# L0's attention as one pipeline over all 64 heads, with double buffers and normalizations on ScalarE

## The reference, cut to what matters

```python
a  = tanh(einsum('ble,hde->blhd', emb, Wa_w) + Wa_b)
bg = einsum('ble,hde->blhd', emb, Wb_w) + Wb_b
# for each head and feature, over the tokens of a sequence:
h  = a[t] * h + bg[t]                     # hs, starts at 0 for each sequence
Dx  = emb @ D_w.T + D_b
out = (einsum('blhd,hkd->blhk', hs, C_w) + C_b) * Dx
out = layernorm(out) * hn_g + hn_b        # per head and token
sum_heads = (Dx + einsum('h,blhd->bld', head_w, out)) / nH
z = sum_heads @ Wout_w.T + Wout_b
u = z + layernorm(z) * norm_g + norm_b
h_out = u + gelu(u @ ffn1_w.T + ffn1_b) @ ffn2_w.T + ffn2_b
y = h_out @ proj_w.T + proj_b             # added to x
```

## Time and profile before

| | us |
|---|---|
| median of three runs | 1402.25 |
| lowest and highest | 1392.26, 1405.36 |
| the profiled execution | 1405.92 |
| its span, first to last instruction | 1404.2 |
| PE, DVE, ACT, POOL busy in the span | 1120.8, 932.8, 672.8, 614.1 |
| mean granted TensorE clock | 0.875 |

### The profile page before, as it was taken

How to read it: one execution, slowest core, us unless ns; L and a number is a source line. 1 busy time by engine, 2 the same in 40 slices (tenths; PEclk the granted TensorE clock), 3 DMA queues, 4 the chain that set the end, 5 groups by cost and what they waited for, 6 DMA issues and landing times. The chain is left out here.

```text
span 1404.2 us, 17282 instructions
## 1 busy us (share of the span) xinstructions
PE 1120.8 (80%) x4972; PEld 814.7 (58%) x4972; DVE 932.8 (66%) x2659; ACT 672.8 (48%) x1242; POOL 614.1 (44%) x695
## 2 busy tenths in 40 slices
PE   5767999966787888798776756899992777999997
PEld 4645878854555565565553545788881444555553
DVE  6647887756787777777754634877773368676662
ACT  3324767743344445345342212677770434455532
POOL 5763000016866776674551754100006466664340
PEclk8659999997999999999996667999996589899997
DMA  7537467731000000000000110577751000000000
GB/s 241 189 113 278 143 209 246 245 100 27 12 12 10 12 11 12 10 12 1 1 1 1 38 38 32 178 226 247 239 196 54 23 18 16 23 23 12 8 8 23
DMA packets 48959, 115.43 MB, mean 82 GB/s; under 512 B 8160, under 2 KB 14304, under 8 KB 48864
## 3 DMA queue, kind: packets, MB, share of 16 engines
q1 hardware_dynamic: 40672, 97.53, 21.3%
q0 software_dynamic: 8192, 16.79, 4.0%
HBM read 79.16 MB, written 35.13 MB: 81 GB/s over the span
## 5 line engine op out<-in xcount | busy, mean ns | idle before, releaser
L642 DVE TENSOR_TENSOR hid_lo<-hid,hid_hi 128x512 fp32r<-128x512 f32 x248 | 170.4, 689 | 102.5 <-ACT hid L442 91.4
L491 POOL DMA_INDIRECT xs<-spare_all,slots x128 | 131.5, 1027 | 72.9 <-issue 36.5
L521 POOL DMA_INDIRECT got<-ys,y_slots x64 | 74.8, 1169 | 199.8 <-DMA ys<-spare_all 183.2
L1068 DVE TENSOR_TENSOR_SCAN spare_all<-spare_all,carry 128x512 f32<-128x512 f32 x64 | 90.9, 1420 | 71.3 <-ACT spare_all L972 67.0
L982 ACT ACTIVATE gate_b<-bank,head_rstd 128x128 f32<-128x128 f32 x256 | 72.9, 369 | 126.4 <-POOL head_rstd L1022 124.5
L442 ACT ACTIVATE hid<-bank,b_up_of 128x512 f32<-128x512 f32 x184 | 125.5, 682 | 6.0
L219 PEld LDWEIGHTS bank<-ident,spare_all 128*128 128x128 f32 x568 | 78.2, 157 | 82.8 <-issue 74.5
L219 PE MATMUL bank<-ident,spare_all 128*128 128x128 f32 x568 | 96.3, 302 | 33.2 <-DVE spare_all L551 13.7
L441 ACT ACTIVATE hid_hi<-bank,b_up_of 128x512 fp32r<-128x512 f32 x138 | 95.1, 689 | 44.8 <-PE bank L364 34.6
L908 PE MATMUL bank<-spare_all,cw_sb 128*128 128x512 f32 x128 | 71.6, 642 | 33.4 <-DVE spare_all L1075 33.4
L1029 POOL TENSOR_TENSOR t_sb<-t_sb,gate_b 128x512 f32<-128x512 f32 x64 | 87.8, 1373 | 0.6
(11 more groups left out here) (267 smaller groups left out, 3020.3 us busy)
## 6 DMA issues: line engine op xcount, KB each, us to landing
wr<-wq SPq DMA_DIRECT2D x92, 512.0 KB, 4.4
spare_all<-xs SPq DMA_DIRECT2D x46, 256.0 KB, 4.6
ys<-spare_all SPq DMA_DIRECT2D x46, 256.0 KB, 4.9
wq<-wr SPq DMA_DIRECT2D x16, 512.0 KB
got<-in_w_mlp SPq DMA_DIRECT2D x9, 512.0 KB
xs<-X SPq DMA_DIRECT2D x16, 256.0 KB
xs<-spare_all,slots POOLq DMA_INDIRECT x128
out_x<-X SPq DMA_DIRECT2D x8, 256.0 KB, 2.3
```

Of the source, the lines that this page charges most:

```text
L491: g.indirect_dma_start(out=xs, out_offset=bass.IndirectOffsetOnAxis(ap=slots[:, k, n:n + 1], axis=0), in_=xn_all[:, n], in_offset=None).th ...
L521: nc.gpsimd.indirect_dma_start(out=rows_of(i, ring)[:, k, b], out_offset=None, in_=ys, in_offset=bass.IndirectOffsetOnAxis(ap=y_slots[:, k ...
L642: v.tensor_tensor(hid_lo[:, q], hid[:, n % HC], hid_hi[:, q].bitcast(F32), ALU.subtract).then_inc(s["lo_done"], 1)
L1068: v.tensor_tensor_scan(hs[:, n % 2], a_sb[:, n % 2], b_sb[:, n % 2], carry[:, n:n + 1], ALU.mult, ALU.add).then_inc(s["hs_ready"], 1)
```

## The change

`turn_of` with its eleven slots is gone. One loop over `MIX_SLOTS` = 64 + 13 slots runs on each engine, and head q = 8 i + h is projected in slot q whatever its tile. Each slot holds the work of heads n, n-1, n-2 and n-3. The work of a tile hangs on `phase` = n % 8, for the tile itself, the one before it, and the one two before (f2, h, y and X of tile i-2 now stand in phases 0 to 4 of tile i).

- Two buffers for `x_hi`/`x_lo` (the halves of `xh` and `xl`), `dx` and `z`.
- x's and z's normalization move from DVE to ACT (`normalize`, `normalize_z`: scale and bias in one instruction for a block). POOL makes the bias with two more small operations in `root`.
- The rows zrow and proj_b come into bank 6 by a matmul with two partitions (`by_token`, `mix_rows`), made at the start by DVE. z's base is copied by ACT (`keep_base`), no longer added by DVE; X has one add instead of two; norm_b is the bias of uT's eviction (a new column `nb`).
- The carry is kept only in the first tile of a sequence, and the other starts from `no_carry`.
- The combine of the next tile is split over phases 0 and 1, ahead of `o_of_head` and the scan. It stood in slot 5.
- In ACT's slot the share stands in front of tanh, and `normalize_z` between them in phase 4. In POOL's slot the add stands in front of the root.
- Only `mix_` functions, the column and the removed `ln_` helpers are touched.

```diff
...
-        dx = part
+        dx = [part[:], xT[:]]
...
-        z = t1[:].rearrange("p (b e) -> p b e", b=TB)
+        z = [t1[:].rearrange("p (b e) -> p b e", b=TB), pick[:].rearrange("p k n e -> p (k n e)").rearrange("p (b e) -> p b e", b=TB)]
...
+        mix_rows = hid_hi[0:2, 5:7]
...
-        SLOTS = NH + 3
-        AB_CREDIT, HS_CREDIT, O_CREDIT, SHARE_CREDIT, ADD_CREDIT, STATS_CREDIT = 2, 1, 1, 2, 2, 1
+        HEADS = NH * TILES
+        MIX_SLOTS = HEADS + NH + 5
+        DX, BASE, TAKE, UN, TURN_U = 0, 2, 4, 4, 5
+        UP_AT, DOWN_AT, H_AT, Y_AT, ADD_X = (6, 7), (0, 1), 2, 3, 4
+        def mix_tiles(n):
+            i = n // NH
+            return [j if 0 <= j < TILES else None for j in (i, i - 1, i - 2)]
...
+            def by_token(row, src, w):
+                nc.tensor.matmul(bank[6][:], mix_sign, mix_rows[:, row], start=True, stop=False, skip_group_check=True)
+                for b in range(TB):
+                    ins = nc.tensor.matmul(blk(bank[6], b), blk(src, b), w, start=False, stop=(b == TB - 1), skip_group_check=True)
+                return ins
...
+            def project_head(q):
+                i, h = divmod(q, NH)
+                if h == 0:
+                    pe.wait_ge(s["x_lo_ready"], i + 1)
+                for k, w in enumerate((wa_parts, wb_parts)):
+                    if q > 0:
+                        pe.wait_ge(s["ab_out"], 2 * q - 1 + k)
+                    project(bank[k], [half[:, h] for half in w], i % 2).then_inc(s["ab_in"], 1)
+            def c_of_head(q):
+                pe.wait_ge(s["hs_ready"], q + 1)
+                if q > 0:
+                    pe.wait_ge(s["o_ready"], q)
+                nc.tensor.matmul(bank[2][:], cw[:, q % NH], hs[:, q % 2], start=True, stop=True).then_inc(s["c_in"], 1)
...
+            for n in range(MIX_SLOTS):
+                phase = n % NH
+                tile, before_it, two_before = mix_tiles(n)
+                if 0 <= n - 2 < HEADS:
+                    turn_head(n - 2)
+                if n < HEADS:
+                    project_head(n)
+                if phase == DX and tile is not None:
+                    dx_of(tile)
+                if 0 <= n - 1 < HEADS:
+                    c_of_head(n - 1)
+                if 0 <= n - 2 < HEADS:
+                    out_of_head(n - 2)
+                if phase in DOWN_AT and two_before is not None:
+                    down(two_before, phase)
+                if phase == BASE and tile is not None:
+                    base(tile)
+                if phase == Y_AT and two_before is not None:
+                    y_of(two_before)
+                if phase == TAKE and n // NH + 1 < TILES:
+                    take_tile(tile + 1)
+                if phase == TURN_U and before_it is not None:
+                    turn_u(before_it)
+                if phase in UP_AT and before_it is not None:
+                    up(before_it, phase - UP_AT[0])
...
+            def share_head(q):
+                act.wait_ge(s["head_rstd"], q + 1)
+                act.wait_ge(s["p_in"], q + 1)
+                if q >= 2:
+                    act.wait_ge(s["added"], q - 1)
...
+            def normalize(i):
+                act.wait_ge(s["rstd_ready"], i + 1)
+                if i > 0:
+                    act.wait_ge(s["xn_turned"], i)
+                for b in range(TB):
+                    ins = nc.scalar.activation(xn[:, b], X[:, i * TB + b], ACT.Identity, bias=shift_x[:, b:b + 1],
+                                               scale=rstd[:, b:b + 1])
+                ins.then_inc(s["xn_ready"], 1)
...
+            def normalize_z(i):
+                act.wait_ge(s["z_rstd"], i + 1)
+                if i > 0:
+                    act.wait_ge(s["u_in"], i)
+                for b in range(TB):
+                    ins = nc.scalar.activation(u[:, b], z[i % 2][:, b], ACT.Identity, bias=z_shift[:, b:b + 1],
+                                               scale=z_rstd[:, b:b + 1])
+                ins.then_inc(s["un_ready"], 1)
...
+            for n in range(MIX_SLOTS):
+                phase = n % NH
+                tile, before_it, two_before = mix_tiles(n)
+                if 0 <= n - 3 < HEADS:
+                    share_head(n - 3)
+                if phase == UN and before_it is not None:
+                    normalize_z(before_it)
+                if n < HEADS:
+                    keep_head(n)
+                if phase == 3 and n // NH + 1 < TILES:
+                    normalize(tile + 1)
+                if phase == DX and tile is not None:
+                    keep_dx(tile)
+                if phase == BASE and tile is not None:
+                    keep_base(tile)
+                if phase == TAKE and n // NH + 1 < TILES:
+                    keep_x(tile + 1)
+                if phase == TURN_U and before_it is not None:
+                    keep_u(before_it)
+                if phase in UP_AT and before_it is not None:
+                    gelu(before_it, phase - UP_AT[0])
...
+            def root(mean, var, var_eps, rstd, shift):
+                steps.link(g.tensor_scalar(var_eps[:], var, EPS, None, ALU.add))
+                steps.link(g.tensor_tensor(rstd[:], var_eps[:], neg_half[:, 0:TB], ALU.pow))
+                steps.link(g.tensor_tensor(shift[:], mean, rstd[:], ALU.mult))
+                return g.tensor_scalar(shift[:], shift[:], -1.0, None, ALU.mult)
...
+            def head_root(q):
+                pool.wait_ge(s["o_stats"], q + 1)
+                if q > 0:
+                    pool.wait_ge(s["head_rstd"], q)
+                if q >= 2:
+                    pool.wait_ge(s["share_ready"], q - 1)
+                steps.link(g.tensor_scalar(head_var[:], o_mv[:, q % 2, :, 1], EPS, None, ALU.add))
+                g.tensor_tensor(head_rstd[:, q % 2], head_var[:], neg_half[:, 0:TB], ALU.pow).then_inc(s["head_rstd"], 1)
+            def add_head(q):
+                i, h = divmod(q, NH)
+                if h == 0:
+                    pool.wait_ge(s["base_out"], i + 1)
+                if q > 0:
+                    pool.wait_ge(s["added"], q)
+                pool.wait_ge(s["share_ready"], q + 1)
+                g.tensor_tensor(z[i % 2], z[i % 2], share[:, q % 2], ALU.add).then_inc(s["added"], 1)
...
+                    x_root(0)
+            for n in range(MIX_SLOTS):
+                phase = n % NH
+                tile, before_it, two_before = mix_tiles(n)
+                if 0 <= n - 3 < HEADS:
+                    add_head(n - 3)
+                if 0 <= n - 2 < HEADS:
+                    head_root(n - 2)
+                if phase == 2 and n // NH + 1 < TILES:
+                    x_root(tile + 1)
+                if phase == 3 and before_it is not None:
+                    z_root(before_it)
+                if n // NH + 2 < TILES and phase < TOP * TB:
+                    moe_fetch(pool, moe, tile + 2, phase, FETCHED)
...
+            def scan_head(q):
+                i, h = divmod(q, NH)
+                dve.wait_ge(s["ab_out"], 2 * q + 2)
+                if i % 2 == 1 and h == 0:
+                    steps.wait()
+                first = no_carry[:, 0:1] if i % 2 == 0 else carry[:, h:h + 1]
+                v.tensor_tensor_scan(hs[:, q % 2], a_sb[:, q % 2], b_sb[:, q % 2], first, ALU.mult, ALU.add).then_inc(s["hs_ready"], 1)
...
+            def u_of(i):
+                dve.wait_ge(s["un_ready"], i + 1)
+                steps.link(v.tensor_tensor(u[:], u[:], ng_row.unsqueeze(1).broadcast_to([P, TB, P]), ALU.mult))
+                v.tensor_tensor(u[:], u[:], z[i % 2], ALU.add).then_inc(s["u_ready"], 1)
...
+            steps.link(v.memset(no_carry[:], 0.0))
+            rows_at = (zrow[0:2], projb_row[0:2])
+            v.tensor_scalar(mix_sign, ident[0:2, 1:2].broadcast_to([2, P]), 2.0, -1.0, ALU.mult, ALU.add)
+            for k in range(2):
+                ins = v.tensor_copy(mix_hi[:, k], rows_at[k])
+            steps.link(ins)
+            for k in range(2):
+                ins = v.scalar_tensor_tensor(mix_rows[:, k].rearrange("r (b e) -> r b e", e=P),
+                                             rows_at[k].unsqueeze(1).broadcast_to([2, TB, P]), ident[0:2, 1:2],
+                                             mix_hi[:, k].bitcast(F32).unsqueeze(1).broadcast_to([2, TB, P]), ALU.mult, ALU.subtract)
+            ins.then_inc(s["rows_ready"], 1)
+            combine(0, 0)
+            combine(0, 1)
+            x_stats(0)
...
+            for n in range(MIX_SLOTS):
+                phase = n % NH
+                tile, before_it, two_before = mix_tiles(n)
+                if 0 <= n - 2 < HEADS:
+                    head_stats(n - 2)
+                if phase in (0, 1) and n // NH + 1 < TILES:
+                    combine(tile + 1, phase)
+                if phase == H_AT and two_before is not None:
+                    h_of(two_before)
+                if phase == ADD_X and two_before is not None:
+                    add_to_x(two_before)
```

(13 more changed lines are left out.)

440 lines of the change are left out of this document (181 added, 259 removed).

## The result

The changed kernel takes 1362.87 us (median of 4 runs, 1359.64 to 1363.67) beside 1402.25 for the kernel before (median of three runs; a fourth, disturbed, took 3601.7 and is left out): ratio 0.9731, 95% interval 0.9668 to 0.9793. It is 2.7% faster, some 39 us. The forecast was 1351 and 51 us.

A forecast was written before the change was run, and what follows sets the result against it. Waits bound the attention stage, chiefly a hole between tiles; within tiles PE set the beat. Stage end 340 + 35 + 43 + 218 + 38 + 33 = 707 against 758.1, 51 us less: 1351 us, range 1341 to 1362.

The forecast's parts named there:

- The hole at the end of each tile is filled: Between a tile's last scan and the next tile's first, 15.3 us before; no bubble should be left.
- Lead: Stage start: DVE combines half of tile 1 ahead of scan 0, which starts near 340, not 333.95: a loss of 6.
- The new wait in phase 4: ACT's normalize_z holds back head 4's tanh and scan: 7.96 us after scan 3, of which 2.2 arrive per tile.
- PE sets 5.3 us steps: Within a tile PE sets the beat: 3.58 us a head, 5.30 in slots that also carry two f1 pieces.
- POOL's slot is 4.06 and a tile 36.7: POOL's slot with a fetch takes 4.06 us, its tile 36.7 with both roots, fitting under PE's 39.3.
- Lost scans cost 0.5 a tile: Scans slowed by POOL's adds: 0.68 us each on scans 2, 4 and 5, bounds 0 and 2.0, taken as 0.5.
- ACT's order lets the add finish before scan 4: POOL's add (1.26 us) follows the share and ends within the tanh pair (1.36), before scan 4 starts.
- Rival B: DVE and POOL shut each other out, scans and u passes lose 0.45 on average: tile 48, 1380 us; chance 0.20.
- Rival C: Ring from head statistics through POOL's root, share, tanh and scan: 6.0 us a head, 1418 us, slower; chance 0.03.
- Rival D: No gain: holes return as DVE's combine waiting for POOL's eighth fetch, time within 1%; chance 0.03.
- Rival A: The z chain is hidden and scans lose nothing: 19 us more gained, 1332 us; chance 0.12.
- Tile 7 and drain: Tile 7, first scan's start to last scan's end, 38 us; the drain from there to stage end 33 us.

The follow-up runs named there:

- x2: Changed kernel with the next tile's combine, x's statistics, root and normalization one slot later in all tiles: 1366.96 us, ratio 0.9736 to the kernel before.
- x11: x1 with the combine of tile 1, its statistics, root and normalization one slot later, in tile 0 only: 1305.08 us, ratio 0.963 to the kernel before.
- x1: Changed kernel with normalize_z behind keep_head (tanh and gate) in ACT's phase 4: 1347.27 us, ratio 0.9645 to the kernel before.
- x4: Changed kernel without POOL's adds of heads 1 to 7, so z is head 0's share alone: 1348.97 us (one run), stage 400.7.
- x15: x11 with POOL's eight fetches per tile spread unevenly over phases 0, 1, 4, 5 and 6: 1347.66 us, ratio 0.9627 to the kernel before.
- x17: Changed kernel with z's normalization back on DVE, in front of u: 1351.91 us, ratio 0.9677 to the kernel before.

## Why the prediction was right or wrong

The time came out 0.9 us above the forecast's own range (1341 to 1362) and well inside 1332 to 1380. In the main the mechanism is right: the hole between tiles is gone, PE sets most steps, and the new wait stands where it was put. The stage was missed by 14.3 us: 6.9 in tile 0, 1.7 in tile 1 and 4.7 in tiles 2 to 5 make 13.3 of them.

- *The hole at the end of each tile is filled*: right. 15.3 became 7 to 8; the forecast had 4.7 from scan 7's end (some 6).
- *Lead*: right, 34.4 for 34. x's root was to end at 326.9 and ended at 329.34, the combine came at 340.91 instead of 338.3, while the stage itself started 1.7 later. That it is a loss is shown by x2 and x11 (29.7).
- *The new wait in phase 4*: right in place and chain. The chain is 7.44 for 7.96, and that the gap between the scans came out at 8.1 to 8.8 all the same is luck: scan 3 was stretched by 0.7 to 1.35 in tiles 1 to 5, and the forecast counted none there. The price of the wait was off too: 2.2 a tile were to arrive, x1 shows 0.5 to 1.4 in steady tiles and 3.0 in tile 6.
- *PE sets 5.3 us steps*: right, as PE's own rows show, though the scans start 4.5 to 5.1 apart. The five steps from head 5 to the next head 2 were to take 26.6. They take 27.0 into tiles 4 and 6; the 0.4 is the base's step, 5.09 for 4.70, in which the bias with two partitions takes 0.42 (527.56 to 527.98), the forecast's other bound. They take 28.0 and 28.1 into tiles 3 and 5, where scan 0 is late and stretched. From head 2 to head 5 the forecast had 16.5; 17.0 came in tiles 2 and 4 and 17.6 in tiles 3 and 5, where scan 3 takes 2.6 instead of 2.0. So 44.8 came for 43.6.
- *POOL's slot is 4.06 and a tile 36.7, "under PE's 39.3"*: **the step that failed** in tile 0. The slot with a fetch is 4.83 to 4.86 where POOL never waits. The 4.06 came from a slot of tile 0 in the kernel before in which no small operation met a scan. I took lost time as a matter of scans alone (0.5 a tile, bounds 0 and 2.0) and gave POOL's small operations none. They lose 0.9 each when they meet a scan: 0.8 a head in tile 0 (4.86 for 4.06), 0.6 a head in the steady tiles (1.88 for 1.27). In tile 0, which the forecast summed from 4.1 a head, this sets the beat. x4 takes 4.7 of the 6.9 us away there; the rest lies in its first four gaps (20.0 for 17.4, in x4 too) and stays open. In the steady tiles PE sets most steps, so POOL's longer slot arrives only in part.
- *Lost scans cost 0.5 a tile*: **the term that was too small** in the steady tiles. The scans of tiles 2 to 5 take 1.7 us a tile more than eight times 1.28. It lands on PE: from head 5's product with C to the next tile's, 43.9 us pass into tile 4, where scan 3 is stretched by 0.7 and scan 0 not, and 45.6 and 45.7 into tiles 3 and 5, where scan 0 is stretched by 1.2 and scan 3 by 1.35. As an estimate, 1.2 more of scans and 0.4 more of the base's step, less the 0.5 by which the chain was shorter, make 1.1 of the 1.2 us that a steady tile is over the forecast. That the adds meet scans 0 and 3 because POOL is late is argued, not shown.
- *ACT's order lets the add finish before scan 4*: true (450.87 and 451.17 in tile 2), but scan 3 meets an add in every tile from 1 to 5. In tile 0 the same order is the reason for the loss. The add is 1.27 and the tanh pair 1.36, so the scan starts exactly when POOL turns to head_var.
- *Rival B* (time lost between DVE and POOL) had the mechanism, with POOL's side left out and the size too large: 48 a tile where 44.8 came. *Rival C* (ring through POOL) is what tile 0 does, with one operation blocked a head and not two: 4.8, not 6.0. *Rival D* (fetch waits) is in the trace: DVE idles 12.3 us in 6 places ahead of a combine. x15 removes these and tiles stay at 44.1 (x11: 43.6 to 45.2): they were a place where POOL's lateness was paid, not a cost of their own. *Rival A* is out.
- *Tile 7 and drain*: 38.7 for 38 and 33.4 for 33, right. *Tile 6* came out 0.5 below the steady tile of the forecast; it has no fetches, and none of its scans is stretched.

The rule of the Trainium skill in SBUF — State Buffer, section "SBUF: two separate sides", says that a VectorE instruction with two SBUF inputs, as the scan is, and a GpSimd instruction that reads SBUF shut each other out: the later one waits for the whole of the other. The trace agrees for POOL's side too, which I had not weighed: 0.23 became 1.15 under a scan that had some 1.1 us left.

The median came out 12 us above the forecast and the stage 14. The whole time follows the stage to some us: x15 has 48.6 less in the median and 50.5 in the stage, x11 50.8 and 46.9, x17 44.4 and 37.1.

Open: in x15 0.3 us a head ((88.20 - 78.47 - 4.3) / 16) lie between POOL's instructions, and no run tells what of it could go. Whether POOL's small operations on another engine would bring the steady tile nearer to PE's beat was not tried, and neither was x1 without the adds, which would show how much of x1's lost gain is POOL's.

## What to carry to other kernels

Once a pipeline has no holes, price each engine's slot again under the new neighbours: an instruction's duration read from a stretch in which it met nothing on the other engine is a lower bound. Two engines that lock each other out and are coupled by a ring settle into a phase; see from the queue order which instruction will start just as the other's long one does, since it pays in every turn. When a wait is taken away and the gap behind it grows, look at all engines in that gap: x1 won 2.3 us in one gap and lost 1.8 in the next, where DVE's queue was full and POOL's root came late. Read the beat from the rows of the engine that is said to set it: the scans here started 4.5 to 5.1 apart in slots in which PE worked 5.3 without a pause.
